# Three one-column products of a fused four-stage kernel move from VectorE to GpSimd

## What is computed

```
x = x + xattn0(layernorm(x), ctx)      # 8 heads, rotary, softmax
x = x + ffn0(layernorm(x))             # three quantised ("bit") linear layers
x = x + xattn1(layernorm(x), ctx, mask)
x = x + ffn1(layernorm(x))             # ternary weights, silu, rms norm

def bit_linear(x, w, b):
    gamma_x = clip(max(abs(x), axis=-1), 1e-05)      # one number per row
    scale_x = 127.0 / gamma_x
    x_dq = clip(round(x * scale_x), -128, 127) / scale_x
    gamma_w = clip(mean(abs(w)), 1e-05)              # one number per matrix
    w_dq = clip(round(w / gamma_w), -1, 1) * gamma_w
    return x_dq @ w_dq.T + b
ffn0 = bit_linear(silu(bit_linear(x, gate)) * bit_linear(x, val), out)
```

## Time and profile before

| | us |
|---|---|
| median of three runs | 824.77 |
| lowest and highest run | 822.72 and 827.39 |
| span of the profiled execution | 828.8 |
| busy in it: PE, DVE, ACT, POOL | 759.6, 739.1, 699.6, 636.2 |

### The profile page before, as it was taken

How to read it: one execution, slowest core, us unless ns; L and a number is a source line. 1 busy time by engine, 2 the same in 40 slices (tenths; PEclk the granted TensorE clock), 3 DMA queues, 4 the chain that set the end, 5 groups by cost and what they waited for, 6 DMA issues and landing times. The chain is left out here.

```text
span 828.8 us, 22129 instructions
## 1 busy us (share of the span) xinstructions
PE 759.6 (92%) x6898; PEld 397.6 (48%) x6898; DVE 739.1 (89%) x1636; ACT 699.6 (84%) x1447; POOL 636.2 (77%) x1139
## 2 busy tenths in 40 slices
PE   2588999999999999999999999999999999998876
PEld 1233344444455554555555555555554545444444
DVE  3898798999999999999999999999999999987765
ACT  3788987988899898999898989999998888887644
POOL 3765656778898888988888888888888887777632
PEclk9555898999999999999999999999999999999999
DMA  8410222344434444544445444444444445434230
GB/s 287 140 54 19 71 67 64 76 105 94 112 87 108 109 110 110 108 116 112 104 111 116 112 101 110 109 105 106 117 101 120 99 91 115 95 87 91 57 72 20
DMA packets 197952, 82.59 MB, mean 100 GB/s; under 512 B 139710, under 2 KB 196670, under 8 KB 197836
## 3 DMA queue, kind: packets, MB, share of 16 engines
q1 hardware_dynamic: 193260, 74.63, 38.5%
q10 hardware_dynamic: 4576, 6.55, 2.4%
HBM read 28.15 MB, written 4.69 MB: 40 GB/s over the span
## 5 line engine op out<-in xcount | busy, mean ns | idle before, releaser
L1141 DVE TENSOR_REDUCE mx<-psS 128x2 f32<-128x512 f32 x512 | 334.1, 680 | 21.8 <-PE psS L630 20.2
L813 ACT ACTIVATE prob<-psT 128x512 f32<-128x512 f32 x512 | 292.5, 604 | 27.0 <-PE psT L638 21.6
L630 PE MATMUL psS<-KQ 31*128 31x256 f16 x1024 | 137.6, 285 | 7.0 <-DVE mx L1141 3.6
L652 PE MATMUL psW<-prob,vst 128*32 128x256 f32 x2048 | 143.0, 400 | 0.1
L741 PE MATMUL psW<-guT,xT 128*128 128x512 bf16 x512 | 132.6, 387 | 6.2 <-DMA xT<-stage 5.3
L638 PE MATMUL psT<-KQ 32*128 32x256 f16 x1024 | 130.4, 280 | 4.0 <-ACT prob L813 3.1
L652 PEld LDWEIGHTS psW<-prob,vst 128*32 128x32 f32 x2048 | 55.0, 112 | 61.4 <-issue 34.6
L741 PEld LDWEIGHTS psW<-guT,xT 128*128 128x128 f16 x512 | 43.1, 99 | 71.5 <-issue 36.5
L1025 POOL TENSOR_TENSOR hqB<-wide,rnd 128x512 bf16<-128x512 f32 x60 | 63.1, 1056 | 13.6 <-ACT wide L863 13.4
L1039 POOL TENSOR_TENSOR stage<-stage 128x512 f16<-128x512 f32 x60 | 69.7, 1162 | 2.5 <-ACT stage L924 1.8
L630 PEld LDWEIGHTS psS<-KQ 31*128 31x128 f16 x1024 | 40.4, 93 | 64.2 <-DVE mx L1141 38.0
(11 more groups left out here) (191 smaller groups left out, 1779.1 us busy)
## 6 DMA issues: line engine op xcount, KB each, us to landing
KQ<-hl SPq DMA_DIRECT2D x192, 64.0 KB, 1.9
xP<-in_x SPq DMA_DIRECT2D x32, 128.0 KB, 2.3
cP<-in_ctx SPq DMA_DIRECT2D x32, 128.0 KB, 2.1
xA<-in_x SPq DMA_DIRECT2D x32, 128.0 KB, 2.7
cB<-in_ctx SPq DMA_DIRECT2D x32, 128.0 KB, 2.3
oV<-uA SPq DMA_DIRECT2D x32, 128.0 KB, 2.1
out<-x SPq DMA_DIRECT2D x32, 128.0 KB, 2.0
oR<-rden_d SPq DMA_DIRECT2D x120, 32.0 KB
```

The lines of the kernel that those rows point to most:

```text
L630: m = nc.tensor.matmul(psS[:, n % 2, T * k:T * k + T], KQ[p % DEEP][r, 1, g, 128 * k:128 * k + 128], KQ[p % DEEP][r, 0, g, :], start=True, ...
L652: m = nc.tensor.matmul(bank[32 * j:32 * j + 32, :], vst[p % DEEP][:, k, 4 * n + j, :], prob[:, (4 * n + j) % 8, k, :], start=(k == 0), sto ...
L813: m = nc.scalar.activation(flat(prob[:, n % 8, :, :]), psT[:, n % 2, :], ACT.Exp, scale=float(HC) ** -0.5)
L1141: m = nc.vector.tensor_reduce(mx[:, p % 2, :, 4 * (n % 4) + n // 4], psS[:, n % 2, :].rearrange("p (c s) -> p c s", c=NK), AX.X, ALU.max)
```

## The change

The three products leave DVE. Columns 4 and 5 become a new POOL step `gs`, and column 9 a new POOL step `os`. In every table `gs` stands right ahead of `rq` of the same pair; `os` stands right ahead of `hq0` of the same pair for pairs 0 to 29, and in the last turns for pairs 30 and 31 behind `hl1:28` and `hl1:29`, ahead of `rsD`. All other orders are the same; the tables are only wrapped at another width. The readers wait for the new steps: `tB` and `sx` for `gs`, `x2` for `os`. The constant `None` of the DVE form becomes a multiplication by 1.0.

```
     "pool": """... ms:-6 r2:2 rot:2 os:-3 hq0:-3 gs:-2 rq:-2 rs:-4""",
...
                 elif kind == "tB":
                     after(act, "Bg", p, n)
                     if n == 0:
-                        after(act, "sxB", p)
+                        after(act, "gs", p)
...
+                elif kind == "gs":
+                    sc = sB[:, p % 2, :]
+                    after(pool, "sxB", p)
+                    after(pool, "tB", p - 2, 1)
+                    after(pool, "sx", p - 2)
+                    if p == 0:
+                        after(pool, "gv", 0)
+                    nc.gpsimd.tensor_scalar(sc[:, 4:5], sc[:, 1:2], gam_q[:, 0:1], 1.0, ALU.mult, ALU.mult)
+                    m = nc.gpsimd.tensor_scalar(sc[:, 5:6], sc[:, 1:2], sc[:, 1:2], gam_q[:, 1:2], ALU.mult, ALU.mult)
+                elif kind == "os":
+                    sc = sB[:, p % 2, :]
+                    after(pool, "sx", p)
+                    after(pool, "x2", p - 2)
+                    m = nc.gpsimd.tensor_scalar(sc[:, 9:10], sc[:, 6:7], gam_q[:, 2:3], 1.0, ALU.mult, ALU.mult)
...
                 elif kind == "sxB":
...
-                    after(dve, "tB", p - 2, 1)
-                    after(dve, "sx", p - 2)
+                    after(dve, "gs", p - 2)
                     sc = sB[:, p % 2, :]
                     inner(1, nc.vector.tensor_scalar(sc[:, 1:2], sc[:, 0:1], 1e-5, 1.0 / 127.0, ALU.max, ALU.mult))
-                    nc.vector.tensor_scalar(sc[:, 4:5], sc[:, 1:2], gam_q[:, 0:1], None, ALU.mult)
-                    nc.vector.tensor_scalar(sc[:, 5:6], sc[:, 1:2], sc[:, 1:2], gam_q[:, 1:2], ALU.mult, ALU.mult)
                     m = nc.vector.reciprocal(sc[:, 2:3], sc[:, 1:2])
...
                 elif kind == "sx":
                     sc = sB[:, p % 2, :]
                     after(dve, "amH", p)
+                    after(dve, "gs", p)
                     after(dve, "hr", p - 2, 1)
-                    after(dve, "x2", p - 2)
+                    after(dve, "os", p - 2)
                     inner(1, nc.vector.tensor_scalar(sc[:, 6:7], sc[:, 3:4], sc[:, 5:6], 1e-5, ALU.mult, ALU.max))
                     inner(2, nc.vector.reciprocal(sc[:, 7:8], sc[:, 6:7]))
-                    nc.vector.tensor_scalar(sc[:, 9:10], sc[:, 6:7], gam_q[:, 2:3], None, ALU.mult)
...
                 elif kind == "x2":
                     after(dve, "Bd", p)
-                    after(dve, "sx", p)
+                    after(dve, "os", p)
```

More of the change, by code:

```diff
@@ L162 @@
-    "pool": """rsP:0 id:0 r2:0 rot:0 rsP:1 lo:0 qa0:0 r2:1 rsP:2 rot:1 qa1:0 lo:1 qb0:0 rsP:3 r2:2 rot:2 lo:2 qb1:0
-           qa2:0 rsP:4 r2:3 rot:3 lo:3 qb2:0 om:0 rsB:0 xnB:0 r2:4 rq:0 rot:4 xb:0 rsP:5 lo:4 om:1 rsP:6 rsB:1 xnB:1
-           r2:5 hq0:0 rq:1 hq1:0 rot:5 xb:1 rsP:7 lo:5 om:2 rsD:0 xnD:0 rsB:2 xnB:2 r2:6 rot:6 rq:2 rs:0 xb:2 hq0:1
-           hq1:1 lo:6 om:3 rsC:0 xnC:0 xl:0 rsB:3 xnB:3 rsP:8 rsD:1 xnD:1 rq:3 r2:7 rot:7 rs:1 xb:3 hq0:2 hq1:2
-           hl0:0 lo:7 rsC:1 xnC:1 hl1:0 xl:1 om:4 rsD:2 xnD:2 rsB:4 xnB:4 r2:8 ms:0 rsP:9 rq:4 rot:8 rs:2 hq0:3 lo:8
-           hq1:3 xb:4 om:5 rsC:2 xnC:2 rsP:10 hl0:1 xl:2 rsB:5 hl1:1 rsD:3 xnD:3 r2:9 rot:9 xb:5 xnB:5 rs:3 ms:1
-           hq0:4 rq:5 lo:9 hq1:4 om:6 hl0:2 rsC:3 xnC:3 hl1:2 rsP:11 xl:3 rsB:6 xnB:6 r2:10 rsD:4 xnD:4 rot:10 ms:2
-           rq:6 hq0:5 rs:4""",
+           mx14:1 mx15:1 r1:3 ct0:0 mx0:2 mx1:2 mvP:4 bs:0 val:0 mx2:2 mx3:2 cl2:0 mx4:2 mx5:2 mx6:2 rc:0 mx7:2 mx8:2
@@ new lines @@
+           mx9:2 ct1:0 mx10:2 mx11:2 r1:4 mx12:2 mx13:2 mx14:2 mx15:2 bsB:0 mvB:0 bsP:5 mx0:3 mvP:5 ct2:0 mx1:3 amB:0
+           sxB:0 mx2:3 mx3:3 mx4:3 mx5:3 rc:1 mx6:3 mx7:3 mx8:3 mx9:3 mx10:3 mx11:3 aB0:0 bsP:6 mx12:3 r1:5 mx13:3
+           mvP:6 hB0:0 mx14:3 aB1:0 mx15:3 bsB:1 hB1:0 mvB:1 amH:0 mx0:4 sx:0 amB:1 mx1:4 sxB:1 mx2:4 mx3:4 mx4:4
+           fx2:0 rc:2 mx5:4 mx6:4 mx7:4 mx8:4 bsP:7 r1:6 mx9:4 mvP:7 aB0:1 mx10:4 mx11:4 x2:0 mx12:4 mx13:4 bsD:0
+           hB0:1 mx14:4 aB1:1 mvD:0 bsB:2 mx15:4 mvB:2 hB1:1 amH:1 sx:1 mx0:5 amB:2 mx1:5 sxB:2 wx:0 mx2:5 rc:3 mx3:5
@@ new lines @@
+    "pool": """rsP:0 id:0 r2:0 rot:0 rsP:1 lo:0 qa0:0 r2:1 rsP:2 rot:1 qa1:0 lo:1 qb0:0 rsP:3 r2:2 rot:2 lo:2 qb1:0 qa2:0
+           rsP:4 r2:3 rot:3 lo:3 qb2:0 om:0 rsB:0 xnB:0 r2:4 gs:0 rq:0 rot:4 xb:0 rsP:5 lo:4 om:1 rsP:6 rsB:1 xnB:1
+           r2:5 os:0 hq0:0 gs:1 rq:1 hq1:0 rot:5 xb:1 rsP:7 lo:5 om:2 rsD:0 xnD:0 rsB:2 xnB:2 r2:6 rot:6 gs:2 rq:2
+           rs:0 xb:2 os:1 hq0:1 hq1:1 lo:6 om:3 rsC:0 xnC:0 xl:0 rsB:3 xnB:3 rsP:8 rsD:1 xnD:1 gs:3 rq:3 r2:7 rot:7
+           rs:1 xb:3 os:2 hq0:2 hq1:2 hl0:0 lo:7 rsC:1 xnC:1 hl1:0 xl:1 om:4 rsD:2 xnD:2 rsB:4 xnB:4 r2:8 ms:0 rsP:9
+           gs:4 rq:4 rot:8 rs:2 os:3 hq0:3 lo:8 hq1:3 xb:4 om:5 rsC:2 xnC:2 rsP:10 hl0:1 xl:2 rsB:5 hl1:1 rsD:3 xnD:3
+           r2:9 rot:9 xb:5 xnB:5 rs:3 ms:1 os:4 hq0:4 gs:5 rq:5 lo:9 hq1:4 om:6 hl0:2 rsC:3 xnC:3 hl1:2 rsP:11 xl:3
+           rsB:6 xnB:6 r2:10 rsD:4 xnD:4 rot:10 ms:2 gs:6 rq:6 os:5 hq0:5 rs:4""",
@@ L253 @@
-    "pool": """hq1:22 hl0:20 lo:27 rsC:21 xnC:21 xb:23 xl:21 om:24 hl1:20 rsD:22 rsP:29 xnD:22 rsB:24 xnB:24 xb:24 r2:28
-           ms:20 rot:28 rq:24 hq0:23 rs:22 hq1:23 lo:28 om:25 rsC:22 hl0:21 xnC:22 xl:22 hl1:21 rsB:25 rsP:30 rsD:23
-           xnD:23 xnB:25 xb:25 hq0:24 hq1:24 r2:29 rq:25 ms:21 rs:23 rot:29 hl0:22 lo:29 om:26 rsC:23 xnC:23 hl1:22
-           xl:23 rsD:24 xnD:24 r2:30 rsB:26 xnB:26 rsP:31 ms:22 rot:30 xb:26 rq:26 rs:24 lo:30 hq0:25 hl0:23 om:27
-           hq1:25 rsC:24 xnC:24 rsB:27 xl:24 hl1:23 xnB:27 ms:23 rsD:25 xnD:25 hq0:26 hq1:26 r2:31 rq:27 rot:31
-           rs:25 lo:31 om:28 xb:27 rsC:25 xnC:25 hl0:24 rsD:26 xl:25 xnD:26 hl1:24 rsB:28 xnB:28 hq0:27 hq1:27 ms:24
-           rq:28 xb:28 rs:26 hl0:25 rsC:26 xnC:26 om:29 xl:26 rsD:27 xnD:27 hl1:25 rsB:29 xnB:29 xb:29 ms:25 hq0:28
-           hq1:28 rq:29 rs:27 rsC:27 xnC:27 om:30 hl0:26 xl:27 rsD:28 xnD:28 hl1:26 xb:30 rsB:30 ms:26 hq0:29 rq:30
-           rs:28 hq1:29 hl0:27 om:31 hl1:27 rsC:28 xnC:28 rsB:31 xl:28 rsD:29 xnD:29 ms:27 rq:31 rs:29 xb:31 hl0:28
-           rsC:29 xnC:29 xl:29 hl1:28 rsD:30 ms:28 rs:30 rsC:30 hl0:29 hl1:29 rsD:31 ms:29 rs:31 rsC:31 ms:30 ms:31""",
@@ new lines @@
+    "pool": """hq1:22 hl0:20 lo:27 rsC:21 xnC:21 xb:23 xl:21 om:24 hl1:20 rsD:22 rsP:29 xnD:22 rsB:24 xnB:24 xb:24 r2:28
+           ms:20 rot:28 gs:24 rq:24 os:23 hq0:23 rs:22 hq1:23 lo:28 om:25 rsC:22 hl0:21 xnC:22 xl:22 hl1:21 rsB:25
+           rsP:30 rsD:23 xnD:23 xnB:25 xb:25 os:24 hq0:24 hq1:24 r2:29 gs:25 rq:25 ms:21 rs:23 rot:29 hl0:22 lo:29
+           om:26 rsC:23 xnC:23 hl1:22 xl:23 rsD:24 xnD:24 r2:30 rsB:26 xnB:26 rsP:31 ms:22 rot:30 xb:26 gs:26 rq:26
+           rs:24 lo:30 os:25 hq0:25 hl0:23 om:27 hq1:25 rsC:24 xnC:24 rsB:27 xl:24 hl1:23 xnB:27 ms:23 rsD:25 xnD:25
+           os:26 hq0:26 hq1:26 r2:31 gs:27 rq:27 rot:31 rs:25 lo:31 om:28 xb:27 rsC:25 xnC:25 hl0:24 rsD:26 xl:25
+           xnD:26 hl1:24 rsB:28 xnB:28 os:27 hq0:27 hq1:27 ms:24 gs:28 rq:28 xb:28 rs:26 hl0:25 rsC:26 xnC:26 om:29
+           xl:26 rsD:27 xnD:27 hl1:25 rsB:29 xnB:29 xb:29 ms:25 os:28 hq0:28 hq1:28 gs:29 rq:29 rs:27 rsC:27 xnC:27
+           om:30 hl0:26 xl:27 rsD:28 xnD:28 hl1:26 xb:30 rsB:30 ms:26 os:29 hq0:29 gs:30 rq:30 rs:28 hq1:29 hl0:27
+           om:31 hl1:27 rsC:28 xnC:28 rsB:31 xl:28 rsD:29 xnD:29 ms:27 gs:31 rq:31 rs:29 xb:31 hl0:28 rsC:29 xnC:29
+           xl:29 hl1:28 os:30 rsD:30 ms:28 rs:30 rsC:30 hl0:29 hl1:29 os:31 rsD:31 ms:29 rs:31 rsC:31 ms:30 ms:31""",
```

279 lines of the change are left out of this document (135 added, 144 removed).

## The result

The changed kernel takes 837.74 us (median of 4 runs, 832.81 to 840.07), the kernel before 826.08 us in the runs beside it. The ratio is 1.0181, with a 95% interval of 1.0134 to 1.0227: it is slower by 11.7 us by the medians, where the sum said 6.0. The two medians alone have the ratio 1.0141; the ratio on record is larger, and by either the loss is about twice the sum or more.

A forecast was written before the change was run, and what follows sets the result against it. Bound: a closed path through POOL, SP, PE and DVE, 21.26 us, beside DVE's 21.36. Adding 0.69 for products and 0.36 for late transfers gives 22.31, 0.30 over 22.01; 20 turns add 6.0 to 824.8: 830.8 us, range 816 to 842.

The forecast's parts named there:

- the sum: Whole kernel: 20 steady turns, each 0.30 us longer, 6.0 us in all, giving 830.8 us.
- Direction and mechanism: Slower, chance 0.51: DVE's turn of 21.36 us and POOL's closed path of 21.26 us nearly equal, products added to POOL's.
- The second path: Closed path POOL, `qT`, PE, `x2`, DVE's `mvD`, back to `rsD`: 21.26 us, becoming 21.95 us with the products.
- The price of a product on POOL: Each product on POOL costs 0.23 us, read from the `nmP` row; three cost 0.69 us a pair.
- DVE's saving: On DVE, `sxB` gets 0.31 us and `sx` 0.13 us shorter: 0.44 us a pair, leaving a turn of 20.92 us.
- The new waits: Waits of `tB`, `sx`, `x2` and `sxB` for POOL cost nothing in the loop; up to 0.5 us for the last two pairs.
- The mean turn: Steady turn of the loop: 21.95 + 0.36 = 22.31 us, 0.30 us more than 22.01, over 20 turns.
- The allowance for late transfers: Late `hqT` and `qT` transfers on POOL's closed path add 0.2 and 0.16 us, 0.36 us a turn.
- The base of the sum: Profiled span of 828.8 us, 4.0 us above the median of 824.8 us; this difference was carried over unchanged.
- DVE as the bound: Rival, chance 0.19: POOL's added work is hidden, DVE's turn falls to 20.92 us, time 816.0 us.
- Cancelling: Rival, chance 0.20: POOL's idle time at `rsC` and `rsD`, or DVE's relief, offsets the products; 824 to 828 us.
- Dear products: Rival, chance 0.09: each product costs 0.55 us on POOL, 1.26 us a turn more, time 850 us.

The follow-up runs named there:

- first and fourth experiment: One: DVE keeps its products, POOL repeats them into a tile nobody reads, 840.14 us; other: changed kernel with all three products behind `hq1` in the steady turn, 828.95 us.
- the second measurement: The changed kernel itself measured once more against the kernel before: 838.87 us, ratio 1.0142.

## Why the prediction was right, point by point

**Direction and mechanism: right.** Two paths of nearly equal length, and the products on the one that POOL holds. The experiments show it from four sides: the products without readers cost 11.0 us, two of three cost 5.5, all three behind `hq1` cost nothing, and DVE's relief alone gives 3.8. `qT` is issued 0.06 or 0.07 us after `rq` in every steady turn, as forecast; before, it was up to 0.71 us in some. Two other signs did not come: the idle time ahead of `rsC` is 5.1 us and not near zero, and L1228 starts 21.25 to 25.87 us apart in the steady part, where 22.2 to 22.5 was forecast.

**The second path: right in length, wrong in its way out.** The forecast was 21.26 + 0.69 = 21.95 us; the turn from 553.58 to 575.53 takes that. It was to show in `x2` waiting for PE "in most turns instead of five"; `x2` waits 4 times. The path leaves PE by `tB`, `xh` and `xl` instead. The legs that close it are 14.69 us on POOL from `xl` at 558.33 to the end of `rq` at 573.02, 2.56 us from the end of `rq` at 551.02 to `bg`, 1.92 us to `tB` and 2.83 us to `xl`: 22.00 us, or 21.26 without the 0.74 of the products. The kernel before thus had this path at the same length as the one that I summed. That the two agree so well says little: starts summed round one turn give that turn's length along any chain, and what tells them apart is the slack. In this turn `rsD` starts at 560.76, 0.25 us after `mvD` ends at 560.51; where `rsC` really waited for `mvC` before, it started 0.08 us after it. So the summed path had an estimated 0.17 us of slack, and the one by `xl`, 0.07 us behind `xh`, holds the turn. Meeting 21.95 to the hundredth, with a price of 0.69 that was 0.74, is luck. The idle time ahead of `rsC` fell from 18 waits and 9.3 us to 8 and 5.1, and POOL's wait moved to `xl`.

**The price of a product on POOL: nearly right**, 0.74 against 0.69 us. The Trainium skill (GPSIMD Engine Reference, Engine selection) puts GpSimd at about half of VectorE's speed for two-input operations; here the durations are 0.26 to 0.32 us on POOL and 0.21 to 0.27 on DVE, so the factor is not seen. A product reads one column and scalars of the same row, and the ratio of about 1.2 is nearer to what the same row of that page says of one-input operations, about equal.

**DVE's saving: too large**, 0.44 us in the sum. Its turn was not the bound, so nothing hung on it. These are the rows of before around:

```profile
474.54 0.14 DVE L1216 TENSOR_SCALAR sB<-sB 128x1 f32<-128x1 f32 x1
...
474.85 0.27 DVE L1218 TENSOR_SCALAR sB<-sB,gam_q 128x1 f32<-128x1 f32 x1
475.04 0.15 DVE L1219 RECIPROCAL sB<-sB 128x1 f32<-128x1 f32 x1
475.11 0.27 DVE L1254 TENSOR_REDUCE sD<-psW 128x1 f32<-128x128 f32 x1
```

From the first of `sxB` to the next step it was 475.11 - 474.54 = 0.57 us and is 569.51 - 569.13 = 0.38 now: 0.19 us saved, not 0.31. I had counted only up to the reciprocal, and what follows it now starts 0.21 us behind it rather than 0.07. `sx` did save the 0.13 us, 0.69 us before and 0.56 now up to its next step. Together that is 0.32 us, so a turn of DVE without waits is an estimated 21.04 us and not 20.92.

**The new waits: right**, nothing in the loop (first and fourth experiment). Where the pipeline empties, `x2` waits for `os` of the last two pairs, 0.6 us in two waits, where up to 0.5 was allowed.

**The mean turn: the term that was mis-sized.** The sum had 22.31 us in 20 turns. Sixteen turns run from the `bg` at 259.25 to that at 620.65 us, 361.40 / 16 = 22.59 us; before, the same sixteen took 352.27 us (259.47 to 611.74), 22.02 each. That is 9.1 us, and outside these turns the two spans differ by -0.3. The allowance for late transfers was cut from 22.01 - 21.36 = 0.65 us a turn to 0.36, because the waits of `aC` for ACT were counted as gone. They grew from 7.2 to 9.5 us, and the allowance came out as 22.59 - 21.97 = 0.62. The second profile of the changed kernel has a mean turn of 22.49 us, and that of the products without readers 22.39, so it is 0.4 to 0.6 us by these three. Two turns stand out in the profile after. These are their first and last `bg`, and the clock in them (PEclk stands ahead of the DMA share and the rate at the end of a window's row):

```profile
437.21 0.37 PE L697 MATMUL psW<-brow,xqT 6*128 6x512 bf16 x1 [1.60 <-DMA xqT<-xqB]
...
461.27 0.38 PE L697 MATMUL psW<-brow,xqT 6*128 6x512 bf16 x1
...
483.54 0.37 PE L697 MATMUL psW<-brow,xqT 6*128 6x512 bf16 x1 [0.87 <-DMA xqT<-xqB]
...
508.80 0.37 PE L697 MATMUL psW<-brow,xqT 6*128 6x512 bf16 x1 [0.28 <-DMA xqT<-xqB]
...
437.00:438.00 1.00, 0.79 (x5) 0.53 (x6) 0.34 (x1) 0.54 (x2) 0.91 (x1) 0.85 1.10 211
438.00:439.00 1.00, 1.00 (x4) 0.81 (x3) 0.44 (x2) 0.00 (x0) 0.40 (x2) 0.50 0.35 85
...
495.00:500.00 5.00, 4.14 (x23) 1.34 (x24) 2.86 (x7) 1.59 (x5) 4.55 (x8) 0.66 0.78 154
```

They take 24.06 and 25.26 us, 5.4 us more than two undisturbed ones, and in both PE ran at its half level for some 3 us after it had stood idle. Without these 5.4 us the mean turn is 22.25 us, close to the 22.31 of the sum. But the kernel before has two long turns as well, 23.57 us from the `bg` at 303.16 and 23.93 us from that at 391.42, without such a fall, so the falls are not shown to be the difference. Whether the change makes them more frequent is open: between 200 and 700 us the clock fell three times in this profile, once in the second one and never in that of the kernel before, but the mean clock of the six runs of the second measurement is 0.953, and that of the eleven runs of the kernel before beside them 0.955, with single runs from 0.946 to 0.967.

The products without readers are 9.6 us slower by the spans of the profiles. The sixteen turns account for 6.0 us, without a fall in them, and the first 260 us and the emptying of the pipeline for 1.9 and 1.8 more, which I had set to nothing. The first of these two is one turn, from the `bg` at 235.78 to that at 261.36 us: 25.58 us, before 22.95. The clock fell in it:

```profile
249.00:251.00 2.00, 2.00 (x11) 0.55 (x13) 0.54 (x4) 0.60 (x1) 1.84 (x4) 0.50 1.28 169
```

The other 1.8 us stay open.

**The base of the sum.** In every run on record the time is 1.8 us above the span of the same execution. By that the profiled execution of the kernel before took an estimated 830.6 us, 4.5 above the median of 826.08; that of the changed kernel took 839.44, 1.7 above its own. I read the mean turn of 22.01 us from a slower execution than most and carried the 4.0 us over unchanged. So the spans differ by 8.8 us and the medians by 11.7: some 2.8 of the 5.7 us that the sum lacks come from there, and the rest from the sixteen turns.

**What I left out: cover.** The sum treats a late transfer as a fixed 0.36 us a turn. The run with the products between `rq` and `rs` loses 1% on a path that the estimate there puts at 20.9 us without the products, below the others, and at 21.7 with them, above. Part of the loss may simply be that it is now the longest. The rest would be cover: a path below the bound still swallows late transfers, and work put on it takes that away. No run separates the two, so this is argued and not shown.

**The rivals.** DVE as the bound (816.0 us) is refuted by the result: DVE lost 0.32 us a turn, and the turn grew by 0.74 with `bg` waiting for `qT`. The relief alone refutes the price of 8.8 us; but with the 0.31 to 0.32 us that DVE really saves the rival would give an estimated 5.0 to 6.4 us in 16 to 20 turns, and the interval of that run, 1.7 to 6.5 us, holds this. The Trainium skill (Perfetto Trace Analysis, Identifying the Most-Contended Engine) would have the fullest engine optimised first; DVE was the fullest at 98%, and taking 0.3 us a turn from it for nothing gave 3.8 us. Cancelling (824 to 828 us) would need POOL's idle time to help in the same turn; the undisturbed turn of 21.95 us says it does not. The 0.23 us at `rsD` that I counted there is no idle time of POOL: the earlier trace rows shows none. Dear products are refuted by their 0.74 us.

## What to carry to other kernels

In a pipeline tuned by hand, look for closed paths, not for the fullest engine: sum the legs of one turn from an instruction back to itself, through every queue, each leg read where its reader really waits, and compare the sums. Here the moved work cost its full length in every undisturbed turn of the path that sets the pace, and nothing on POOL's stretch behind the last hand-off of that path; the same three products cost 1.4 to 1.8% ahead of `hq0` and `rq` and nothing behind `hq1`. A path somewhat below the bound may not be free either: its distance from the bound would be what absorbs late transfers, which one run suggests. And set the span of the profile that you sum from against the median of the runs first: ours was a slow execution, and its waits went into the sum.

## What was not expected of the hardware

PE stood idle for 1.60 us ahead of the `bg` at 437.21, and the granted clock fell to 0.50 from 438 to 441 us, the half level of 1.2 GHz. An idle time of 1.76 us ahead of the `bg` at 217.18 was followed by no fall (1.00 from 215 to 220 us). The fall in the second long turn (0.50 from 496 to 499 us) came behind two shorter ones, 0.94 us ahead of 493.50 and 0.95 us ahead of 495.86. The length of one idle stretch does not decide it.
